# Separate order tables for the start, the middle and the end of a 32-tile Trainium2 kernel, with its setup made part of tile 0

## The reference

```python
x = x + xattn(_layernorm(x), ctx, Wq, Wk, Wv, Wo, bo)   # 16 heads of 64, ctx is 64 x 128 x 96
x = x + attn(_layernorm(x), Wp, bp, Wv, Wo)             # causal, 16 heads
x = x + ffn(_layernorm(x), Wq, bq, K1, K2, W_up, W_down)

# attn: similarity of two positions from 5 sigmoid "path" bits a head
agree = pq * pk + (1.0 - pq) * (1.0 - pk)
sim = jnp.cumprod(agree, axis=-1).sum(axis=-1) / Dt      # then causal mask and softmax

# ffn: product keys, top 10 of 32 x 32 pairs for each of 8 heads, then the experts of those pairs
v1, i1 = jax.lax.top_k(s1, TOPK); v2, i2 = jax.lax.top_k(s2, TOPK)
vals, best = jax.lax.top_k(all_scores, TOPK)
h = jnp.einsum('bsd,bshkd->bshk', x, W_down[expert_idx])
h = jax.nn.gelu(h, approximate=False) * softmax(vals)
out = jnp.einsum('bshk,bshkd->bsd', h, W_up[expert_idx])
```

## Time and profile before

| | us |
|---|---|
| median of 3 runs | 1033.04 |
| lowest, highest | 1031.93, 1037.06 |
| the profiled execution | 1040.14 |
| its span, first to last instruction | 1038.3 |

### The profile page before, as it was taken

The page is one execution under the profiler, slowest core; times in us unless marked ns, Lnnn a source line. Parts: engine busy times, 40 slices in busy tenths (PEclk is TensorE's granted clock), DMA queues, the critical chain, the costliest instruction groups (busy, mean ns, idle before and its releaser), DMA issues.

```text
span 1038.3 us, 35741 instructions
## 1 busy us (share of the span) xinstructions
PE 962.4 (93%) x12440; PEld 771.7 (74%) x12440; DVE 844.8 (81%) x2813; ACT 878.9 (85%) x2157; POOL 838.7 (81%) x841
## 2 busy tenths in 40 slices
PE   3878999999999999999999999999999999999764
PEld 2667777778877787778887887778887877778533
DVE  2236788888988888889988988888998888888773
ACT  1366899999999999999999999999999999999652
POOL 1122888988889888888899888988899888988766
PEclk9699999999999999999999999999999999999875
DMA  6000110011101110111101110011111110000000
GB/s 178 13 6 21 25 26 14 19 27 28 27 24 28 27 28 9 25 28 28 28 23 28 27 24 18 20 27 27 28 25 26 27 29 16 16 21 21 14 16 6
DMA packets 70367, 27.25 MB, mean 26 GB/s; under 512 B 47312, under 2 KB 69936, under 8 KB 70192
## 3 DMA queue, kind: packets, MB, share of 16 engines
q1 hardware_dynamic: 69152, 24.58, 10.1%
q10 hardware_dynamic: 1040, 0.39, 0.2%
HBM read 14.47 MB, written 2.10 MB: 16 GB/s over the span
## 4 chain that ended last, share of the span: by engine, by line
PE 50%; ACT 20%; DVE 15%; issue 11%; POOL 2%; SPq 1%; DMA 1%; POOLq 0%; DVEq 0%; ACTq 0%
ACT p L691 12%; PE psXT L435 8%; PE psF L580 8%; PE psXT L415 7%; PE psXT L395 5%; ACT ew L790 4%; DVE mw L992 3%; DVE cand L966 3%; ACT am L733 3%; PE psXT L321 3%; PE psXT L417 3%; PE psXT L605 2%; PE psXT L322 2%; PE psXT L323 2%; DVE best L961 2%
## 5 line engine op out<-in xcount | busy, mean ns | idle before, releaser
L1115 POOL TENSOR_TENSOR wsum<-wsum,mw 128x1024 f32<-128x1024 f32 x192 | 453.3, 2361 | 6.6 <-DVE mw L992 1.4
L992 DVE SCALAR_TENSOR_TENSOR mw<-psF,cut,ew 128x1024 f32<-128x1024 f32 x256 | 324.0, 1277 | 13.9 <-ACT ew L790 8.9
L790 ACT ACTIVATE ew<-psF,lnz 128x1024 f32<-128x1024 f32 x256 | 282.2, 1115 | 19.3 <-PE psF L580 16.5
L1056 POOL TENSOR_TENSOR p<-p,rrow 128x512 f32<-128x512 f32 x128 | 132.1, 1042 | 74.9 <-DVE rrow L889 74.9
L691 ACT ACTIVATE p<-psXT,negmax 128x128 f32<-128x128 f32 x512 | 178.9, 375 | 5.4 <-DVE negmax L880 5.2
L580 PE MATMUL psF<-sel,usT 128*128 128x512 f16 x512 | 157.1, 390 | 22.9 <-DVE mw L992 21.1
L372 PE MATMUL psXT<-cT,q 96*128 96x128 f32 x1024 | 140.3, 281 | 1.4 <-ACT p L691 1.4
L372 PEld LDWEIGHTS psXT<-cT,q 96*128 96x128 f32 x1024 | 128.1, 194 | 8.7 <-ACT p L691 1.6
L880 DVE TENSOR_REDUCE negmax<-psXT 128x4 f32<-128x512 f32 x128 | 87.2, 681 | 37.9 <-PE psXT L372 37.9
L691 ACT ACTIVATION_READ_ACCUMULATOR p<-psXT,negmax 128x1 f32 x512 | 111.4, 218 | 0.0
L415 PE MATMUL psXT<-pT,c 128*32 128x384 f32 x768 | 110.7, 503 | 0.8 <-ACT pT L616 0.8
(11 more groups left out here) (135 smaller groups left out, 2272.2 us busy)
## 6 DMA issues: line engine op xcount, KB each, us to landing
cT<-cT_dram SPq DMA_DIRECT2D x32, 96.0 KB, 2.0
c<-c_dram SPq DMA_DIRECT2D x32, 96.0 KB, 2.1
x<-x_dram SPq DMA_DIRECT2D x32, 64.0 KB, 1.9
xr<-x_dram SPq DMA_DIRECT2D x32, 64.0 KB, 1.8
y_dram<-y SPq DMA_DIRECT2D x32, 64.0 KB, 1.8
wqT<-wqT_dram SPq DMA_DIRECT2D x1, 512.0 KB, 4.9
wo<-wo_dram SPq DMA_DIRECT2D x1, 512.0 KB, 6.8
wdT<-wdT_dram SPq DMA_DIRECT2D x1, 512.0 KB, 3.4
```

What stands on the lines that cost most here:

```text
L790: done(f"e.x{h}", act.activation(ew[:, h % NEW, :], at(f"e.s{h}"), ACT.Exp, bias=lnz[:, t % 4, h:h + 1]))
L992: done(f"e.w{h}", dve.scalar_tensor_tensor(out=mw[:, h % NMW, :], in0=at(f"e.s{h}"), scalar=cut[:, t % 4, h:h + 1], in1=ew[:, h % NEW, :], ...
L1056: done(f"x.n{k}", pool.tensor_tensor(p[:, k, :, :], p[:, k, :, :], rrow[:, k, :].unsqueeze(2).to_broadcast([128, 4, M]), ALU.mult))
L1115: done(f"e.a{h}", pool.tensor_tensor(wsum[:, t % 2, :], mw[:, 0, :] if h == 1 else wsum[:, t % 2, :], mw[:, h % NMW, :], ALU.add))
```

## The change

1. **Tables.** Each engine has three: FILL for turns 0 to 4, ORDER for turns up to 30, DRAIN from turn 31 on. `run` keeps for each step a counter of the tiles done; in each turn it brings the step up to the turn's number minus its lag, with as many tiles as that takes. The order in the middle turns is changed too, at about ten places.
2. **Setup as steps.** `s.vo`, `a.vo`, `s.keys`, `a.keys`, `d.keys`, `d.bias` and `d.down` have their own semaphores and places in the FILL tables. `s.vo` now stands ahead of the first queries; `d.keys` stands ahead of `y.res` of tile 0. `d.down` waits for the load of wdT alone.
3. **WARM.** 48 matmuls of ones16 by ones16 into a bank that is not read, ahead of the wait for wqT, wkT and ident.
4. **Banks and waits.** Seven steps change their bank (`t.out` from 3 to 6, `x.p1`, `x.q3` and `e.out` among them). The `at_ends` waits are gone; the waits on the readers of the new banks are written for all tiles or for one tile (`t == 31`).
5. **Chains.** The semaphores inside a step count on instead of being worked out from the tile's number. `a.open` and `a.close` load their tables only in turns that have a tanh or a gelu.

```diff
+WARM = 48
-                for name, lag in order.items():
-                    t = i - lag
-                    if (name, t) in once:
-                        once[name, t]()
-                    if 0 <= t < NT + longer.get(name, 0) and (name, t) not in begun:
-                        steps[name](t)
+                lags = fill if i < FILL_TURNS else drain if i >= NT - DRAIN_TURNS else order
+                upto = {name: min(i - lag, 0 if name in ONCE else NT - 1) for name, lag in lags.items()}
+                tanh = any(todo[name] <= upto[name] for name in TANH if name in lags)
+                for name in lags:
...
+                    while todo[name] <= upto[name]:
+                        steps[name](todo[name])
+                        todo[name] += 1
...
+            pe.wait_ge(own["dve_parts"], 4)
+            for _ in range(WARM):
+                pe.matmul(psXT[:, 3, 0:128], ones16[:], ones16[:], start=True, stop=True)
             pe.wait_ge(own["wqk_load"], 16 * 3)
...
             def tree_out(t):
+                after(pe, "a.vo", 0, t == 0)
+                after(pe, "e.w1", t - 1, t == 1)
+                after(pe, "e.gate", t - 2)
...
                     elif h == 3:
+                        after(pe, "t.res", t + 1)
+                        after(pe, "e.w1", t, t == 0)
                         after(pe, "e.gate", t - 1)
-                        at_ends(pe, "e.w1", t)
...
             def experts_out(t):
-                after(pe, "y.res", t + 3)
-                at_ends(pe, "t.res", t + 2)
-                at_ends(pe, "e.add", t - 1)
+                after(pe, "x.w2", t + 4)
...
-            def setup_down():
-                dve.wait_ge(own["expert_load"], 16 * 3)
+            def setup_down(t):
+                dve.wait_ge(own["down_load"], 16)
...
+DVE_FILL = {
+    "t.res": 6, "x.r1": 4, "e.gate": 6, "k.low": 5, "e.w2": 5, "x.r3": 4, "e.w3": 9, "x.low": 3, "d.keys": 4,
...
+FILL_TURNS, DRAIN_TURNS = 5, 1
```

More of the change, by code:

```diff
@@ L607, in _ @@
             steps["e.out"] = experts_out
-            run(steps, PE_ORDER, once={PE_VO: setup_vo, PE_KEYS: setup_keys})
+            run(steps, PE_FILL, PE_ORDER, PE_DRAIN)
         def pairs(j, w, rows):
@@ L795, in _ @@
             for j in range(4):
[L796 removed]
+                act.wait_ge(own["qk_ps"], j + 1)
                 act.activation(qk16[:, 0, 4 * j:4 * j + 4, :].rearrange("p (i e) c -> p e i c", e=2), pairs(j, CD, D),
[L798 to L800 removed]
+                               ACT.Copy, scale=QKSCALE).then_inc(own["qk_sb"], 1)
@@ L1139 @@
+    "a.close": 4, "t.v": 3,
 }
 DVE_ORDER = {
[4 rows of a table removed]
+    "e.w2": 6, "e.w1": 6, "x.stats": 2, "x.x1": 4, "e.w0": 6, "x.r2": 4, "x.x3": 4, "x.r1": 4, "t.div": 5,
+    "e.gate": 7, "t.res": 5, "x.r3": 4, "e.w5": 6, "x.low": 3, "k.low": 5, "e.w3": 6, "e.w4": 6, "k.top": 5,
+    "e.w6": 6, "k.split": 5, "y.res": 4, "k.cand": 5, "x.x0": 3, "e.w7": 6, "k.z": 5, "e.add": 7, "x.r0": 3,
+    "x.w3": 3, "x.x2": 3,
 }
 POOL_ORDER = {
-    "k.cut": 6, "e.a7": 7, "x.norm": 2, "x.n0": 4, "x.n2": 4, "x.n1": 4, "e.a1": 6, "k.norm": 5, "x.n3": 4,
@@ new lines @@
+ACT_DRAIN = {
[3 rows of a table added]
+    "k.shift": 4, "x.w0": 2, "x.w2": 2, "x.w1": 2, "a.open": 0, "t.sb": 3, "e.gelu": 4, "t.path": 3,
+    "a.close": 9, "t.v": 3,
+}
+DVE_DRAIN = {
+    "t.div": 6, "e.gate": 8, "t.res": 6, "e.w5": 7, "x.r3": 5, "x.low": 4, "k.low": 6, "e.w3": 7, "e.w4": 7,
+    "k.top": 6, "k.split": 6, "e.w6": 7, "y.res": 5, "k.cand": 6, "x.x0": 4, "e.w7": 7, "k.z": 6, "x.r0": 4,
+    "e.add": 8, "x.w3": 4, "x.x2": 4, "e.w2": 6, "e.w1": 6, "x.r2": 4, "x.stats": 3, "x.x1": 4, "x.x3": 4,
+    "e.w0": 6, "x.r1": 4,
+}
```

325 lines of the change are left out of this document (168 added, 157 removed), and 35 rows, old and new, of tables (ACT_DRAIN, ACT_FILL, ACT_ORDER, BANK).

## The result

The changed kernel takes **1020.65 us** (median of 4, 1018.76 to 1021.89) against 1034.6 us of the kernel before beside it (median of 4, 1031.93 to 1037.06): a ratio of 0.9875, with a 95% interval of 0.9852 to 0.9898. It is faster, by 14 us. I had said 1007.5 us, in a range from 994 to 1017; the direction was right, and the time lies 13.1 us above the forecast and outside the range.

A forecast was written before the change was run, and what follows sets the result against it. It took the filling's order and low clock as the loss, the steady middle being nearly full on PE and ACT. Terms -14.7, -7.5, -0.5, -2.8 and 0 sum to -25.5 us: 1033.04 becomes 1007.5 us, range 994 to 1017.

The forecast's parts named there:

- What bounds the kernel: Whole span: middle periods even and full at 29.18 us; the filling of 56 us is lost to order and low clock.
- Tile 0, -14.7: Up to the first `y.out`: reordered setup, earlier `x.s0` and WARM matmuls save 14.7 us, bounds 10 to 21.
- Period of tile 1, -7.5: First to second `y.out`: PE's 5.07 us wait for actx, `setup_keys` and low clock go; 7.5 us saved, bounds 4 and 9.
- Steady, -2.8: 28 middle periods: earlier `t.cturn` saves 0.1 us each, new waits taken as 0; 2.8 us saved, bounds -13 to +7.
- End, 0: Behind the last `y.out`: order hardly moves, so no change, bounds -2 to +3 us.
- From the profile to the median: Whole time: the profiled execution's 7.1 us above the median of 1033.04 us is taken off the changed kernel too.
- The steady table adds a wait: Rival, middle periods: `t.feat` and new bank waits meet, +0.25 instead of -0.1 us a period; 1017 us, chance 0.12.
- It doesn't do what it says: Rival, filling: another wait replaces that for `x.low`; only -11 us, 1022 us, chance 0.06.
- The first `y.out` at 41 us: Sign, tile 0: first `y.out` at 41 us; 36 if setup ran fast, 46 if only the block went.
- the second 25 us later: Sign, tile 1: second `y.out` about 25 us behind the first, with no wait of PE for actx.
- Neither sign of being wrong: Wrong if the steady period is 29.4 us or more, or PE waits for a load in the first 40 us.

The follow-up runs named there:

- e11: Kernel before with the statistics step `x.stats` one turn later in DVE's row, for all tiles: 1027.31 us, ratio 0.9917.
- e7: Kernel before with only the setup of the keys moved, on PE, ACT and DVE: 1030.61 us, ratio 0.9937.
- e14: The changed kernel, unchanged, profiled a third time: 1019.77 us, first `y.out` at 40.98 us.
- first profile: The changed kernel, unchanged, as first profiled: 1018.76 us, first `y.out` at 37.20 us.
- e3: Changed kernel with 68 more matmuls into an unread bank, in PE's gaps in the period of tile 1: 1018.83 us, ratio 0.9836.
- e4: Changed kernel with `t.feat` ahead of `e.a6` again in POOL's steady table: 1020.27 us, ratio 0.9855.

## Why the forecast missed, by its own steps

- **What bounds the kernel: right.** The fill was the place, and the order of `x.low`, `setup_vo` and the keys the cause (e11, e7).
- **Tile 0, -14.7: right in its order, with luck in the rest.** The order was worth 11.6 us (e11) where I had 10.1. The rest was between 3.4 (e14) and 7.2 us (first profile), for 4.6 in the sum; no run parts the clock from the earlier `x.s0` in it, and e14 came to -15.0 although the WARM matmuls, of which I counted 0.8, did not raise the clock there. The range of -10 to -21 held it.
- **Period of tile 1, -7.5: wrong, and the largest miss of the terms.** It gave 0.7 us. I took the drop of the clock in before as the result of the 5.07 us of idleness and let it vanish with them. It fell twice all the same, first behind a wait of 2.12 us: 5.2 us (e3). As what is late next I had named ACT's last exponential, at 0.3 us; what came was `t.norm` on POOL, whose wait of 1.30 us the change itself had made 2.12, and 0.79 and 0.73 us behind it. The remaining 1.6 us are the 24.6 us period that is 26.25 at full clock, 0.8 of them this longer wait.
- **Steady, -2.8: the two halves were right in kind, and one too small.** -2.4 for the other edits of the middle turns (e4 against before) and +2.5 for `t.feat` behind `e.a6`. The 0.26 us that `t.cturn` now waits was in neither. I saw that the cover was smaller than the add, priced the difference at 0.05 us, and then took 0.
- **End, 0: right to within its own scatter**, 70.7 to 73.3 us in three profiles of the same kernel.
- **From the profile to the median: wrong, 7.1 us, more than all terms together.** I took the profile's excess over the median as something that the changed kernel would have too. The profile was of one of the slowest executions, at a low clock; the three profiles of the changed kernel lie at its median, so nothing carried over. The forecast for the changed kernel's profile would have been 1014.6 us; the three profiles average 1020.6. Some 6 us of the 13.1 are the terms above, 7.1 us are this.
- **The rivals.** "The steady table adds a wait" was the mechanism that came, at 0.1 us a period instead of 0.25, and it had 0.12. "It doesn't do what it says" gave 1022 us, nearest to the result, by another cause. The upper end of the range should have held a fill in which the clock falls again: 6 us more, 1023.
- **The signs.** The first `y.out` at 41 us came only in e14, and the second 25 us later only with fillers (25.8 to 26.4). Neither sign of being wrong came: the steady period is 817.72 / 28 = 29.20 us, and in the first profile PE waits for no load before 40 us. Neither looked at the clock in the period of tile 1.
